# Another order of pieces within a tick in four stages of a decoder kernel

## The reference

```
x = _layernorm(x + _L1_xattn_ref(x, ctx_2048, ctx_2048, gamma))     # position attention
...
x = _layernorm(x + _L2_attn_ref(x, w_qkv, w_swiglu, w_out))         # cumulative attention
x = _layernorm(x + _L2_xattn_ref(64, 64, 256, w, u, x, ctx_2048))   # decayed attention
...
x = _layernorm(x + _L3_xattn_ref(x, ctx_2048, mask, ...))           # context attention
```

## Time and profile before

| | before |
|---|---|
| median of 3 runs | 4915.02 (4914.43 to 4915.18) |
| profiled execution, its own time | 4917.29 |
| its span | 4915.3 |
| PE busy | 4447.4 (90%) |
| DVE busy | 3261.4 (66%) |
| ACT busy | 2048.8 (42%) |
| POOL busy | 1522.7 (31%) |

### The profile page before, as it was taken

How to read it: one execution, slowest core, us unless ns; L and a number is a source line. 1 busy time by engine, 2 the same in 40 slices (tenths; PEclk the granted TensorE clock), 3 DMA queues, 4 the chain that set the end, 5 groups by cost and what they waited for, 6 DMA issues and landing times.

```text
span 4915.3 us, 87683 instructions
## 1 busy us (share of the span) xinstructions
PE 4447.4 (90%) x32598; PEld 3090.8 (63%) x32645; DVE 3261.4 (66%) x6084; ACT 2048.8 (42%) x4390; POOL 1522.7 (31%) x3050
## 2 busy tenths in 40 slices
PE   8998998799989898887799999999978999999788
PEld 6776887455546676776466666666655666666555
DVE  5667227788877678877555555555546666666798
ACT  4554113355544333333355555555533434343222
POOL 1111004433312233433344444444422222222122
PEclk9999998899999999999899999999999999999899
DMA  1003001344410100000000000000010000000000
GB/s 44 2 25 91 1 1 24 95 88 88 88 43 25 73 7 7 7 9 6 31 1 1 1 1 1 1 1 1 1 42 18 9 7 9 7 9 4 6 14 17
DMA packets 117700, 111.69 MB, mean 23 GB/s; under 512 B 22368, under 2 KB 110112, under 8 KB 112800
## 3 DMA queue, kind: packets, MB, share of 16 engines
q1 hardware_dynamic: 117280, 106.09, 8.3%
HBM read 88.48 MB, written 16.78 MB: 21 GB/s over the span
## 4 chain that ended last, share of the span: by engine, by line
PE 58%; issue 15%; DVE 15%; POOL 7%; ACT 4%; DMA 1%; SPq 1%; POOLq 0%; DVEq 0%; ACTq 0%
PE banks L2421 14%; PE banks L1279 5%; PE banks L2671 4%; PE banks L769 4%; POOL factors L2883 3%; PE banks L1910 3%; PE banks L1262 3%; PE banks L1155 2%; PE banks L2487 2%; PE banks L798 2%; PE banks L2587 1%; PE banks L1816 1%; PE banks L523 1%; PE banks L2515 1%; POOL mean_squares L2879 1%
## 5 line engine op out<-in xcount | busy, mean ns | idle before, releaser
L282 POOL TENSOR_TENSOR var_eps<-mean_var,ln_eps 128x1 f32<-128x1 f32 x384 | 83.3, 217 | 1309.2 <-DVE mean_var L278 959.3
L1319 ACT ACTIVATE exps<-banks 128x512 f32<-128x512 f32 x512 | 284.9, 595 | 259.1 <-PE banks L1262 258.9
L1167 DVE TENSOR_REDUCE neg_max<-banks 128x4 f32<-128x1024 f32 x256 | 311.2, 1217 | 98.4 <-PE banks L1155 98.1
L2442 ACT ACTIVATE squares<-banks 128x512 f32<-128x512 f32 x256 | 152.8, 597 | 441.4 <-PE banks L2421 441.4
L2475 DVE TENSOR_TENSOR q_normed<-banks,factors 128x512 f32<-128x512 f32 x256 | 176.3, 689 | 229.6 <-POOL factors L2465 229.3
L2859 ACT ACTIVATE squares<-q_normed 128x512 f32<-128x512 f32 x160 | 100.8, 630 | 396.6 <-DVE q_normed L2849 396.6
L2465 POOL TENSOR_TENSOR factors<-mean_squares,minus_half 128x4 f32<-128x4 f32 x256 | 258.5, 1010 | 21.5 <-POOL mean_squares L2461 0.3
L1910 PEld LDWEIGHTS banks<-yT,w_swiglu 128*128 128x128 f32 x2048 | 238.0, 193 | 30.0 <-issue 29.8
L1910 PE MATMUL banks<-yT,w_swiglu 128*128 128x128 f32 x2048 | 247.2, 277 | 8.4 <-DVE hidden L1934 8.4
L2421 PE MATMUL banks<-wq,x_turned 128*128 128x512 f32 x512 | 249.0, 609 | 3.0 <-ACT x_turned L2401 1.9
L284 POOL TENSOR_TENSOR rstd<-var_eps,minus_half 128x1 f32<-128x1 f32 x384 | 242.0, 630 | 30.1
(11 more groups left out here) (381 smaller groups left out, 11050.2 us busy)
## 6 DMA issues: line engine op xcount, KB each, us to landing
contextT<-in_ctxT SPq DMA_DIRECT2D x96, 128.0 KB, 2.5
parts_context<-parts SPq DMA_DIRECT2D x96, 64.0 KB, 2.2
parts_x<-parts SPq DMA_DIRECT2D x96, 64.0 KB, 2.0
stack<-parts_context SPq DMA_DIRECT2D x32, 192.0 KB
stack<-parts_x SPq DMA_DIRECT2D x32, 192.0 KB
x_all<-in_x SPq DMA_DIRECT2D x1, 4096.0 KB, 14.2
context<-in_ctx SPq DMA_DIRECT2D x64, 64.0 KB, 2.2
context<-in_ctx SPq DMA_DIRECT2D x32, 128.0 KB, 2.3
```

Source lines behind the costliest of these rows:

```text
L1167: v.tensor_reduce(self.mx[s][:, :, 2 * i:2 * i + 2].rearrange("p h g -> p g h"), self.bM[i % 2].rearrange("p g (h c) -> p g h c", h=DH), A ...
L1319: self.nc.scalar.activation(self.e[n % 8][:], self.bE[self.slot(t, n) % 2].rearrange("p (l c) -> p l c", l=DH), ACT.Exp, scale=self.TOK ** ...
```

## The change

No arithmetic is changed, and no operation is added or removed. Four tables are re-laid, one function is cut in two, and three waits change.

- Position attention: `turn_max_pe` and `copy_max_act` now come first within their turn, ahead of the score and of the exponential.
- Cumulative attention: all pieces get new ticks. The gates lie at 12, 13, 15 and 16 (10 to 13 before), the output halves at 17 and 19 (14 and 15), `turn_y` at 11 (7), and projection at 2 (1). `y_dve` is cut into `den_dve` at 9 and `y_dve` at 10. Bank 0 is now taken in another order: `turn_x` of the next tile comes ahead of `turn_y` of this one, and the waits of both follow that.
- Decayed attention: everything is 2 ticks later (`FIRST`), and `y_dve(0)` and `y_dve(1)` only 1 and 0.
- Context attention: within a tick DVE now sums squares, then scales, then adds the bias; before it was bias, scale, sum.

```
-            "pe": [[(6, self.weigh_last_pe), (5, self.score_late_pe), (4, self.score_from_pe), (4, self.turn_max_pe), (3, self.max_pe)]],
-            "act": [[(5, self.exp_late_act), (4, self.exp_act), (4, self.copy_max_act)]],
+            "pe": [[(4, self.turn_max_pe), (6, self.weigh_last_pe), (5, self.score_late_pe), (4, self.score_from_pe), (3, self.max_pe)]],
+            "act": [[(4, self.copy_max_act), (5, self.exp_late_act), (4, self.exp_act)]],
...
# CumulativeAttention.turn_x_pe
-            pe.wait_ge(self.yT_ready.sem, self.yT_ready.all(t - 1))
+            if begun(t - 2):
+                pe.wait_ge(self.yT_ready.sem, self.yT_ready.all(t - 2))
+            pe.wait_ge(self.xT_ready.sem, self.xT_ready.all(t - 1))
...
# CumulativeAttention.turn_y_pe
-        pe.wait_ge(self.xT_ready.sem, self.xT_ready.all(t))
+        pe.wait_ge(self.xT_ready.sem, self.xT_ready.all(Tile(min(t.index + 1, self.NT - 1))))
+        if begun(t - 1):
+            pe.wait_ge(self.yT_ready.sem, self.yT_ready.all(t - 1))
...
+    GATES = (12, 13, 15, 16)
...
-            "pe": [(5, self.past_pe)] + [(10 + c, self.gate_pe(c)) for c in four] +
-                  [(14 + i, self.out_pe(i)) for i in two] + [(7, self.turn_y_pe), (0, self.turn_x_pe), (1, self.project_pe)],
-            "act": [(7, self.turn_y_act), (0, self.turn_x_act), (0, self.square_x_act), (1, self.square_act), (4, self.exp_act)] +
-                   [(10 + c, self.gate_act(c)) for c in four] + [(17, self.scale_act)],
-            "dve": [(4, self.weighted_dve), (16, self.stats_dve)] + [(11 + c, self.gate_dve(c)) for c in four] + [(6, self.y_dve)],
-            "pool": [(2, self.scales_pool), (16, self.tail_shift_pool)],
+            "pe": [(at, self.gate_pe(c)) for c, at in gates] + [(0, self.turn_x_pe), (8, self.past_pe), (17, self.out_pe(0)), (2, self.project_pe),
+                   (11, self.turn_y_pe), (19, self.out_pe(1))],
+            "act": [(at, self.gate_act(c)) for c, at in gates] + [(11, self.turn_y_act), (0, self.turn_x_act), (21, self.scale_act), (2, self.square_act),
+                    (0, self.square_x_act), (6, self.exp_act)],
+            "dve": [(at + 1, self.gate_dve(c)) for c, at in gates] + [(20, self.stats_dve), (7, self.weighted_dve), (9, self.den_dve), (10, self.y_dve)],
+            "pool": [(3, self.scales_pool), (20, self.tail_shift_pool)],
...
# DecayedAttention
-    FIRST = 20
+    FIRST = 22
...
-                   [(at + 9, self.y_dve(0)), (at + 11, self.y_dve(1)), (at + 12, self.y_dve(2))],
+                   [(at + 8, self.y_dve(0)), (at + 9, self.y_dve(1)), (at + 12, self.y_dve(2))],
...
# ContextAttention
-            "dve": [(chunk + u, self.bias_dve(u)) for u in range(6)] + [(chunk + 2 + u, self.scale_dve(u)) for u in normed] +
-                   [(chunk + 1 + u, self.sum_squares_dve(u)) for u in normed] + [(self.SCORES, self.mask_dve), (self.SOFTMAX, self.softmax_dve),
+            "dve": [(chunk + 1 + u, self.sum_squares_dve(u)) for u in normed] + [(chunk + 2 + u, self.scale_dve(u)) for u in normed] +
+                   [(chunk + u, self.bias_dve(u)) for u in range(6)] + [(self.SCORES, self.mask_dve), (self.SOFTMAX, self.softmax_dve),
```

More of the change, by code:

```diff
@@ L1861, in weighted_dve, with den_dve @@
         self.nc.vector.scalar_tensor_tensor(self.ww[:, 0, :], self.bV[:, 0:D], self.rx[s][:, 0:1], self.ww[:, 1, :], ALU.mult, ALU.mult).then_inc(self.weighted.sem, 1)
-    def y_dve(self, dve, t, s):
+    def den_dve(self, dve, t, s):
         v = self.nc.vector
@@ L1869, in y_dve @@
         link(v.reciprocal(self.rden[:], self.den[:]))
+    def y_dve(self, dve, t, s):
+        link = Links(dve.wait_ge, self.y_steps, t)
+        link.k = 2
         if begun(t - 1):
             dve.wait_ge(self.y_turned.sem, self.y_turned.all(t - 1))
-        link(v.tensor_tensor(self.y[:], self.bC[:, 0:D], self.rden[:], ALU.mult))
+        link(self.nc.vector.tensor_tensor(self.y[:], self.bC[:, 0:D], self.rden[:], ALU.mult))
         link.close()
@@ L1958, in scale_act @@
         self.tail_scale_act(act, t, s, self.bY[:, 0:D])
+    GATES = (12, 13, 15, 16)
     def programs(self):
-        four, two = range(4), range(2)
+        gates = list(enumerate(self.GATES))
         return {
-            "pe": [(5, self.past_pe)] + [(10 + c, self.gate_pe(c)) for c in four] +
-                  [(14 + i, self.out_pe(i)) for i in two] + [(7, self.turn_y_pe), (0, self.turn_x_pe), (1, self.project_pe)],
-            "act": [(7, self.turn_y_act), (0, self.turn_x_act), (0, self.square_x_act), (1, self.square_act), (4, self.exp_act)] +
-                   [(10 + c, self.gate_act(c)) for c in four] + [(17, self.scale_act)],
-            "dve": [(4, self.weighted_dve), (16, self.stats_dve)] + [(11 + c, self.gate_dve(c)) for c in four] + [(6, self.y_dve)],
-            "pool": [(2, self.scales_pool), (16, self.tail_shift_pool)],
+            "pe": [(at, self.gate_pe(c)) for c, at in gates] + [(0, self.turn_x_pe), (8, self.past_pe), (17, self.out_pe(0)), (2, self.project_pe),
[4 more added lines that the diff above has]
+            "pool": [(3, self.scales_pool), (20, self.tail_shift_pool)],
             "sp": [],
```

## The result

| | before | after |
|---|---|---|
| median | 4914.8 | 4874.3 (4870.5 to 4874.5, 4 runs) |
| ratio after to before | | 0.9916 [0.9901, 0.9931] |
| span of the profiled execution | 4915.3 | 4872.6 |
| PE busy | 4447.4 | 4443.3 |

The change makes the kernel 0.84% faster, 40 us, where 104 us were forecast. The time lies outside the range of the prediction.

A forecast was written before the change was run, and what follows sets the result against it. The prediction took PE as the fullest engine, so only its idle time could be won: 19 (position attention) + 46 (context attention) + 39 (C and D) = 104 us off the 4915.0 median, giving 4811 us, range 4786 to 4850.

The forecast's parts named there:

- Position attention: Term: PE's 0.62 us wait for the copy of the maxima goes in 31 tiles, 19 us less.
- Context attention: Term: PE's waits for probabilities and scaled query shrink, 1.47 us in each of 31 tiles, 46 us less.
- C and D: Term for cumulative (C) and decayed (D) attention: period 19.44 to 18.1 us, 41.5 less 2.5 for the ends, 39 us less.
- D's `turn_x` needs C's new x of the same tile: Step in C and D: ACT writes that x behind the second tanh, done 7.6 us after PE's transpose of y.
- PE is there at 6.5 and waits 1.06 us: Step in C and D: PE reaches D's `turn_x` 6.5 us after the transpose of y, making PE's sum 17.6.
- PE's own sum: Step in C and D: PE's pieces together take 16.5 us a tile, without the new wait.
- The ring: Step in C and D: chain from y's transpose through tanh, exponentials, scan and DVE back to y sets the period, 18.1 us.
- The scan beside POOL: Step in C and D: the denominator's scan, starting with POOL's `values_pool`, and two operations behind take 2.53 us, against 1.67.
- The ends of the section: Step in C and D: the pipeline, two ticks deeper, costs at most 4.9 us; 2.5 taken.
- the one in which C and D eat up their gain: Rival, 18%: POOL's scales delay ACT's new x, ring and PE grow, C and D gain nearly nothing; 4842, up to 4850.
- The case called slower: Rival, 3%: D's `turn_x` waits for the new x until C and D's period is 21.5 us; 4925 and more.
- three signs of being wrong: In C and D: scan later than 9.1 us, projection waiting for `weighted` or exponentials, or ends over 5 us longer.

The follow-up runs named there:

- run 1: The kernel before with the change of position attention alone: 4899.7 us, ratio 0.9967 to the kernel before, -15.4 us.
- run 4: The changed kernel with D's last scaling on ACT moved ahead of D's exponentials in the same tick: 4832.3 us, ratio 0.9831 to the kernel before.
- run 9: The changed kernel with three useless products on PE ahead of the waits of D's `turn_x`: 4835.7 us, ratio 0.9836 to the kernel before.
- run 6: The kernel of run 4 with D's transposes of x also one tick later on PE and ACT: 4826.4 us, ratio 0.9813 to the kernel before.
- run 7: The kernel of run 4 with D's product by the values on POOL waiting until DVE has the denominator: 4804.3 us, ratio 0.9769 to the kernel before.
- run 5: The changed kernel with six useless products on PE ahead of the waits of D's `turn_x`: 4901.3 us, ratio 0.9964 to the kernel before.
- run 8: The kernel of run 6 with D's exponentials one tick earlier on ACT, ahead of the second tanh: 4788.5 us, ratio 0.9737 to the kernel before.

## Why the prediction was wrong

**Position attention: right, 15.4 us for 19.** The 0.62 us at L1262 is gone. The idle time of that group fell from 29.0 to 12.4 us in all, 16.6. ACT's share of it fell from 19.4 to 0.2, but the share that ends with the DMA of the stack rose from 8.2 to 10.0. From one transpose of the maxima to the next it was 16.99 us and is 16.40, so 0.59 less, but four tiles are 0.3 to 1.0 us longer than that, where before two were 0.3 to 0.4 longer. From the first to the last it is 15.3 us less, which is what run 1 gained.

**Context attention: right, 47.0 us for 46.** The two waits went, and ACT's copy replaces them, as worked out. The size is in part luck: a period fell from 27.21 to 25.81 us, 1.40 and not 1.47, and another 2.9 us, for which the sum has no term, came from the last step between two tiles, where the section empties.

**C and D: wrong, +20 us for -39.** The step that failed is "D's `turn_x` needs C's new x of the same tile", with its "PE is there at 6.5 and waits 1.06 us". It reads one semaphore of the three on which that piece waits. The wait runs on to D's own new x of two tiles before, behind 1.4 us of exponentials and a scaling: 2.99 us from start to start, 1.9 more than forecast. Run 4 shows it, by taking that scaling ahead. PE's own sum was forecast as 16.5 us a tile and is 19.03 - 2.99 = 16.04 (run 9). With the true wait it would have been 16.5 + 3.0 = 19.5 us, the 19.44 of before, and the forecast for the section no gain.

**The clock: missing from the prediction altogether.** Behind that wait TensorE ran for part of the gates at the lower of its levels (granted clock 0.50 from 2006.1 to 2009.3 us), which cost 1.45 us a tile. So the period is 16.04 + 2.99 + 1.45 = 20.48 us, and no other term is left. Run 9 shows both halves at once, since it takes away the clock's part and leaves the wait. Before, with four waits of 0.29 to 0.55 us, the clock was 1.00.

**The ring: the right mechanism, hidden behind another.** Counted from the transpose of y at 2017.40 - 20.48 = 1996.92, C's second tanh starts at 6.6 us and the denominator's scan at 8.9, where 6.7 and 9.1 had been forecast. The ring is not what sets the period of the changed kernel. It does in run 4, once PE's wait is shorter, as runs 6 and 7 show.

**The scan beside POOL: size right, place wrong.** Forecast were 1.22 for the scan, 0.77 and 0.43 for the two behind it, 2.53 in all; it is 0.70, 0.73 and 0.83, so 2.36. The scan starts 0.05 us ahead of POOL's product and is not lengthened. The product then takes 1.13 where it takes 0.68 alone, and the next two on DVE are lengthened in their turn. The long scan that the prediction took as its model, the last one before, had it the other way round: there POOL's product starts first and keeps its 0.68, and the scan takes 1.21.

```profile
2332.74 0.68 POOL L2097 TENSOR_TENSOR weighted<-key_weight,values 128x256 f32<-128x256 f32 x1 [1.32 <-ACT now_weights L2089]
2332.76 1.21 DVE L2107 TENSOR_TENSOR_SCAN denominator<-decay,key_weight 128x260 f32<-128x260 f32 x1 [1.65 <-ACT now_weights L2089]
```

Both agree with the exclusive use that the Trainium skill describes (SBUF — State Buffer, "SBUF: two separate sides"), including the part that the prediction left out: the operation that starts first isn't held up. Held to the letter, the product of the period shown would end at 2005.79 + 0.70 + 0.68 = 2007.17, and it ends at 2006.97, so the rows bear the rule out to within 0.2 us, and the three operations behind it are as near.

**The ends of the section: sign wrong.** 2.5 us were added for a deeper pipeline. The first turn of D's x stands 37.6 us behind C's first projection, where it stood 43.1 behind it, and the last stands as far from the section's end as before. So the ends gave back 5.5 us. Between them, from D's first turn to its last, the 31 steps cost 622.8 - 597.5 = 25.3, less than 31 times 1.04, since the steps in which the section fills and empties aren't full periods.

**The rival that came nearest** was the one in which C and D eat up their gain, with 18% and 4842 to 4850 us. It had the place, but took POOL's factors as its cause, and they were in time: in the profile after, C's new x starts right behind the tanh. The case called slower, with 3%, named the right wait, D's `turn_x` for a new x, but again by way of POOL. None of the three signs of being wrong that the prediction lists came up: the scan starts at 8.9, the projection doesn't wait, and the ends are shorter. What it expected and did not get is a wait of about 1 us at D's `turn_x`, which is 2.83.

## What to carry to other kernels

When a piece is moved, list every semaphore that it waits for, with the tile of each, and place each signal in the new order of the engine that gives it: the price is set by the last one, and a wait on an older tile comes late when its signal lands in the same tick. Idle time of TensorE isn't only its sum: one wait of 2.83 us cost 1.45 us more behind it, where four of up to 0.55 us cost nothing beyond themselves, and the granted clock of the stretch tells it at a glance. Where operations of DVE and POOL lengthen each other in the chain that sets the period, a wait that keeps them apart may pay, as in run 7.

## What the runs showed of the hardware

- Behind a wait of 2.83 us in each period of 20.48 the granted clock of the section was 0.91 (0.50 from 2006.1 to 2009.3 us), and 32 gate products took 4.98 us instead of 3.74. Behind a wait of 1.76 in 18.77 (run 4) it was 1.00 and 3.74.
- Products whose results nobody reads, put into the idle time, held it at 1.00 (runs 5 and 9), and made the kernel 38.6 us faster when they fit.
- A two-input operation of DVE of 0.42 us took up to 0.83 beside a product of POOL, and the product 1.13 instead of 0.68; a scan started 0.05 us ahead of the product was unchanged, one started 0.02 us behind it took 1.21 (the kernel before), and one started within a product 0.92 instead of 0.70 (run 8).
